# Front adjacency loads issued together, its masks made in place two chunks at a time, and 16 filler transposes left out of a graph attention kernel

## What is computed

```
h = max(layernorm(x), 0)
neib_att = tanh(neigh @ Wn1 + bn1) @ Wn2 + bn2        # 4096 x 32
value    = neigh @ Wv + bv                            # 4096 x 128
x_att    = tanh(h @ Wx1 + bx1) @ Wx2 + bx2            # 4096 x 32
ws  = leaky_relu(x_att @ neib_att.T, 0.01)            # 4096 x 4096
ws  = softmax(where(adj > 0, ws, -9e15), axis=1)
out = x + concatenate([h @ Wfx + bfx, ws @ value], axis=1)
```

## Time and profile before

| what | value |
|---|---|
| median of three runs | 489.14 us (488.77 to 489.36) |
| the profiled execution | 488.76 us |
| its span, first to last instruction | 486.8 us |
| PE, DVE, ACT, POOL busy | 96%, 88%, 84%, 53% of the span |
| granted TensorE clock, mean | 1.00 |

### The profile page before, as it was taken

One profiled execution on the slowest core, in us unless ns is written; L12 is line 12 of the kernel. 1 busy time (PEld: TensorE's weight loads), 2 busy tenths in 40 slices (PEclk: granted clock), 3 DMA queues, 4 the chain that ended last, 5 costly groups with the idle time before them and its releaser, 6 DMA issues.

```text
span 486.8 us, 10746 instructions
## 1 busy us (share of the span) xinstructions
PE 467.1 (96%) x3728; PEld 423.8 (87%) x3728; DVE 426.0 (88%) x852; ACT 410.8 (84%) x586; POOL 258.5 (53%) x361
## 2 busy tenths in 40 slices
PE   7987889999999999999999999999999999999897
PEld 7975679998899989998998989998999989988896
DVE  4678999989989999999999998989999888989654
ACT  2455898899988999899898998899889998999763
POOL 3108147844686457745685458745694555453200
PEclk9999999999999999999999999999999999999999
DMA  8944635557456754566445854476546465551000
GB/s 316 284 91 88 151 66 88 99 93 158 86 88 110 143 104 83 107 123 136 82 95 87 173 100 73 93 140 120 104 78 130 82 110 85 102 95 37 10 12 13
DMA packets 32373, 51.51 MB, mean 106 GB/s; under 512 B 2368, under 2 KB 22976, under 8 KB 32320
## 3 DMA queue, kind: packets, MB, share of 16 engines
q0 software_dynamic: 9216, 33.56, 42.1%
q1 hardware_dynamic: 22816, 17.17, 11.0%
q10 hardware_dynamic: 288, 0.10, 0.1%
HBM read 80.19 MB, written 4.19 MB: 173 GB/s over the span
## 4 chain that ended last, share of the span: by engine, by line
PE 74%; ACT 5%; issue 4%; DVE 4%; POOL 2%; DVEq 0%; ACTq 0%; POOLq 0%
PE ps_turned L936 20%; PE ps_product L957 11%; PE ps_product L959 11%; PE ps_product L958 11%; PE ps_scores L914 10%; PE ps_scores L913 6%; PE ps_product L879 3%; POOL scores L455 2%; ACT scores L551 2%; DVE pt_lo L690 2%; ACT scores L563 1%; PE ps_product L855 1%; ACT pt_hi L525 1%; PE ps_product L871 1%; DVE mask L679 1%
## 5 line engine op out<-in xcount | busy, mean ns | idle before, releaser
L690 DVE TENSOR_TENSOR pt_lo<-ps_turned,pt_hi 128x512 fp32r<-128x512 f32 x256 | 173.5, 686 | 35.3 <-ACT pt_hi L525 23.9
L455 POOL TENSOR_TENSOR scores<-scores,mask 128x512 f32<-128x512 f32 x117 | 136.2, 1164 | 118.6 <-ACT scores L551 118.4
L525 ACT ACTIVATE pt_hi<-ps_turned 128x512 fp32r<-128x512 f32 x256 | 155.4, 607 | 42.6 <-PE ps_turned L936 41.6
L957 PE MATMUL ps_product<-pt_hi,v_hi 128*128 128x256 f32 x512 | 165.0, 322 | 0.1
L936 PE MATMUL ps_turned<-ident,scores 128*128 128x128 f32 x1024 | 154.5, 273 | 2.0 <-DVE pt_lo L690 1.7
L959 PE MATMUL ps_product<-pt_lo,v_hi 128*128 128x256 f32 x512 | 144.3, 282 | 0.0
L958 PE MATMUL ps_product<-pt_hi,v_lo 128*128 128x256 f32 x512 | 144.0, 281 | 0.0
L551 ACT ACTIVATE scores<-ps_scores 128x1024 f32<-128x1024 f32 x128 | 132.1, 1032 | 10.3 <-PE ps_scores L914 10.3
L936 PEld LDWEIGHTS ps_turned<-ident,scores 128*128 128x128 f32 x1024 | 121.2, 140 | 21.6 <-DVE pt_lo L690 3.9
L563 ACT ACTIVATE scores<-scores,neg_top 128x2048 f32<-128x2048 f32 x64 | 129.1, 2018 | 0.0
L708 DVE CUSTOM_DVE_ANT_0 scores<-ps_scores,scores,top 128x1024 f32<-128x1024 f32 x96 | 122.5, 1276 | 1.1 <-ACT scores L551 0.9
(11 more groups left out here) (71 smaller groups left out, 349.4 us busy)
## 6 DMA issues: line engine op xcount, KB each, us to landing
adj_in<-in_adj POOLq DMA_DIRECT2D x60, 512.0 KB, 5.5
scores<-in_neigh_t SPq DMA_DIRECT2D x8, 512.0 KB, 7.7
x_rows<-in_x SPq DMA_DIRECT2D x7, 512.0 KB, 5.7
x_left<-in_x SPq DMA_DIRECT2D x8, 256.0 KB, 5.7
x_right<-in_x SPq DMA_DIRECT2D x16, 128.0 KB, 5.2
scores<-in_adj POOLq DMA_DIRECT2D x4, 512.0 KB, 6.6
out_h<-x_left SPq DMA_DIRECT2D x8, 256.0 KB, 2.4
out_h<-x_right SPq DMA_DIRECT2D x16, 128.0 KB, 2.4
```

The lines of the kernel that those rows point to most:

```text
L455: pool.tensor_tensor(half, half, mask[:, s % MASK_RING, BANK:CHUNK], ALU.add).then_inc(masked, 1)
L525: act.activation(pt_hi[:, (2 * b + u) % HI_RING], pt[:, u], ACT.Copy).then_inc(hi_done, 1)
L690: dve.tensor_tensor(pt_lo[:, u], pt[:, u], pt_hi[:, (2 * b + u) % HI_RING].bitcast(FP32), ALU.subtract).then_inc(lo_done, 1)
L957: pe.matmul(product_of(g), v_hi[:, block, :], high, start=block == 0, stop=False)
```

## The change

The fillers of neighbour steps 1 to 3 are left out. POOL issues the four loads of the front one behind the other once the last neighbour load has landed. The masks of the 8 front chunks are made in place in `adj_front`, two chunks in one DVE instruction, in steps 2, 3, 6 and 8 at the end of DVE's side work. PE and POOL read them there. The mask ring and its counts skip these chunks (`ring_place`). The statistics of group 1 of x come before step 0. Due steps of x's load, normalisation, `x_left`'s load and sums and `x_right`'s sum move. In DVE's step `neigh_rest` comes before `close` (which does nothing before step 14, when `neigh_rest` is over).

```
-FILL = (6, 6, 6, 4, 0, 0, 0, 0)
+FILL = (6, 0, 0, 0, 0, 0, 0, 0)
-X_LOAD = -12
+X_LOAD = -14
 X_STATS = (-6, -6, -6, -4)
 X_AGGR = -2
 X_RSTD = (-2, -2, -1, 0)
-X_NORM = (1, 3, 3, 4)
+X_NORM = (3, 4, 4, 5)
 X_TURN = (6, 8)
...
-X_LEFT_LOAD, X_SUM = 8, (13, 18)
-X_RIGHT = 14
+X_LEFT_LOAD, X_SUM = 7, (16, 19)
+X_RIGHT = 16
...
-AHEAD_STATS = 0
+AHEAD_STATS = -1
+FRONT_MASKS = (2, 3, 6, 8)
...
+        def ring_place(n):
+            return n - FRONT if n >= ADJ_RING else n
+        def made_in_front(n):
+            return ADJ_RING <= n < ADJ_RING + FRONT
+        def mask_of_chunk(n):
+            return adj_front[:, n - ADJ_RING, :] if made_in_front(n) else mask[:, ring_place(n) % MASK_RING, :]
...
             pool.wait_ge(rows_in[NEIGH_GROUPS - 1], 16)
-            load_adj(2 * LOAD)
-            pool.wait_ge(x_ahead_in, 16)
-            load_adj(3 * LOAD)
+            for p in range(FRONT // LOAD):
+                load_adj(ADJ_RING + p * LOAD)
             for i in range(NEWTON + 1):
                 rstd_of(1, i)
-            load_adj(4 * LOAD)
-            load_adj(5 * LOAD)
...
-                    act.wait_ge(mask_done, ADJ_RING + FRONT)
+                    act.wait_ge(masked, ADJ_RING + FRONT - POOL_MASKS)
...
+                if made_in_front(n):
+                    return
...
+            def front_mask(p):
+                dve.wait_ge(front_ready[p], 16)
+                pair = adj_front[:, p * LOAD:(p + 1) * LOAD, :].rearrange("p a n -> p (a n)")
+                dve.tensor_scalar(pair, pair, 0.0, MASKED, ALU.is_le, ALU.mult).then_inc(front_masked, 1)
...
             def x_work(s):
+                for p in range(FRONT // LOAD):
+                    if s == FRONT_MASKS[p]:
+                        front_mask(p)
...
-                    pe.wait_ge(mask_done, k + 1)
+                    if made_in_front(s):
+                        pe.wait_ge(front_masked, (s - ADJ_RING) // LOAD + 1)
+                    else:
+                        pe.wait_ge(mask_done, ring_place(s) + 1)
```

More of the change, by code:

```diff
@@ L201, in build @@
         front_ready = [sem(f"front_ready{i}") for i in range(FRONT // LOAD)]
-        mask_done = sem("mask_done")
+        mask_done, front_masked = sem("mask_done"), sem("front_masked")
         scored = sem("scored")
@@ L442, in step @@
                 if s % LOAD == 0 and n < STEPS and not ADJ_RING <= s < ADJ_RING + FRONT:
-                    pool.wait_ge(mask_done, s + LOAD)
+                    pool.wait_ge(mask_done, ring_place(s) + LOAD)
                     load_adj(n)
@@ L454, in step @@
                     half = scores[:, parity * TILES + tile, c * CHUNK + BANK:(c + 1) * CHUNK]
-                    pool.tensor_tensor(half, half, mask[:, s % MASK_RING, BANK:CHUNK], ALU.add).then_inc(masked, 1)
+                    pool.tensor_tensor(half, half, mask_of_chunk(s)[:, BANK:CHUNK], ALU.add).then_inc(masked, 1)
                 for i in range(NEWTON + 1):
@@ L666, in mask_of @@
             def mask_of(n):
[L668 to L679, removed]
+                if made_in_front(n):
+                    return
+                r = ring_place(n)
+                dve.wait_ge(adj_ready[r % ADJ_RING // LOAD], 16 * (r // ADJ_RING + 1))
+                if r >= MASK_RING:
+                    gone = r - MASK_RING
+                    if gone >= ADJ_RING:
+                        gone += FRONT
+                    dve.wait_ge(scored, gone + 1)
+                    if gone >= POOL_MASKS:
+                        dve.wait_ge(masked, gone + 1 - POOL_MASKS)
+                dve.tensor_scalar(mask[:, r % MASK_RING, :], adj_in[:, r % ADJ_RING, :], 0.0, MASKED, ALU.is_le,
                                   ALU.mult).then_inc(mask_done, 1)
+            def front_mask(p):
+                dve.wait_ge(front_ready[p], 16)
+                pair = adj_front[:, p * LOAD:(p + 1) * LOAD, :].rearrange("p a n -> p (a n)")
+                dve.tensor_scalar(pair, pair, 0.0, MASKED, ALU.is_le, ALU.mult).then_inc(front_masked, 1)
             def lo(s, u):
@@ L775, in step @@
                 negate(s)
+                neigh_rest(s)
                 close(s)
-                neigh_rest(s)
                 x_work(s)
@@ L912, in score @@
                 if not on_pool:
-                    pe.matmul(ps[:, s % 2, half], ident_bf16, mask[:, s % MASK_RING, half], start=True, stop=False)
+                    pe.matmul(ps[:, s % 2, half], ident_bf16, mask_of_chunk(s)[:, half], start=True, stop=False)
                 last = pe.matmul(ps[:, s % 2, half], xs[:, parity, tile * P:(tile + 1) * P],
```

## The result

The changed kernel took a median of 493.31 us (492.57 to 494.38, four executions) against 489.25 us for the kernel before on the same chip: a ratio of 1.0094, 95% interval 1.0081 to 1.0107. It is slower by 0.9%, where 488.7 us and a range of 486.2 to 490.7 were forecast. The moved due steps, which the title doesn't name, decide it. The profiled execution took 492.57 us, 3.81 more than that of before: 3.3 in the span (490.1) and 0.5 around it. (What lies around the span was 1.9 to 2.5 us in the profiled executions of all kernels here; the runs tie it to nothing.)

What follows compares the result with a forecast made beforehand. PE was taken to set the pace from step 12 on. Fillers -0.85, front of the loop -2.0 and due steps +2.4 sum to -0.45 us on 489.14: 488.7 us, range 486.2 to 490.7.

Steps and rivals of the forecast that it cites:

- The due steps of every group: +2.4 us: Main loop: PE waits for POOL's late normalisation at the turn of x, 0.4 us later in each of six groups.
- POOL's chain: POOL from step 4's addition at 201.46 through two additions and three normalisations to 207.46, plus 0.05 signal; PE waits 0.76.
- The 0.35 that comes back: Third step of a group: moving x_left's and x_right's sums on POOL returns 0.35 us that PE lost before a score.
- full price: Rival: the turn of x costs 0.8 us in each of six groups, +1.95 in all, 491.1 us; chance 0.07.
- Fillers, -0.85: Prologue: leaving out 16 filler transposes on PE brings the value layers and first score 0.85 us earlier.
- Loads, 0: Front adjacency loads issued earlier change nothing; x_ahead still lands at 26.5; POOL may be held by a fourth load.
- Front of the loop, -2.0: Early steps: paired masks of 0.7 and earlier normalisation bring x_left's sum forward; 2.0 us passes into the main loop.
- POOL blocks the front masks: Rival: front masks wait for POOL's normalisations, the loop gains nothing, +1.55, 490.7 us; chance 0.12.
- The turn doesn't hold PE: Rival: the turn of x costs PE nothing in the groups, only the front counts, -2.85, 486.3 us; chance 0.30.
- The clock falls: Rival: without fillers PE's clock falls in the prologue, +3 on the forecast, 491.7 us; chance 0.06.
- the dear ends of the last three: Slowest outcomes of the rivals on blocked front masks, the turn's full price and the falling clock, left outside the range.

Runs made afterwards that it cites:

- e9: The kernel before with only x's normalisation moved, to steps 3, 4, 4, 5 of a group: 494.8 us, ratio 1.0122.
- e3: The changed kernel with all due steps of the side work back as before; fillers out, early loads and paired masks stay: 486.92 us, ratio 0.997.
- e4: The kernel before with only the 16 later fillers left out: 487.57 us, ratio 0.9983.
- e7: e5 with the front masks made one chunk at a time instead of two per instruction: 485.85 us, ratio 0.9943.
- e2: The kernel before with only the due steps of the change (x's load and normalisation, x_left's load and sums, x_right's sum): 493.96 us, ratio 1.0107.
- e11: e7 with all 22 fillers of the kernel before: 487.04 us, ratio 0.9965.
- e8: e5 with the four front loads issued as in the kernel before: 487.39 us, ratio 0.9976.
- e1: The changed kernel with x's normalisation alone back in steps 1, 3, 3, 4 of a group: 488.68 us, ratio 1.0003.
- e5: e3 with six fillers again before neighbour step 1: 486.58 us, ratio 0.9961.
- e6: The changed kernel with the turn of x in steps 7 and 9 instead of 6 and 8: 491.25 us, ratio 1.0047.
- e10: The changed kernel with x's normalisation and x_right's sum back in their steps of before: 486.3 us, ratio 0.9953.

## Why the prediction was wrong

**The step that failed** is "The due steps of every group: +2.4 us", a term with the right mechanism and the wrong size: it measured 5.08. The place, PE's pause before the turn of x from e = 2 to 7, ended by POOL's last normalisation, is as forecast, and e9 shows that moving the normalisation alone makes the loss. Both entries of the working were off.

*POOL's chain.* The addition of step 4 started where I had it: 200.93 here is 201.46 in the time of the earlier trace rows, as step 48 comes 0.53 earlier. From there to the end of the last normalisation I summed 6.00 us; it took 6.31, and the signal 0.10 rather than 0.05. The additions are as summed (1.17, 1.16). The normalisations are not: 2.64 for two (1.44 and 1.21) and 1.38, where I took 1.22 each from the earlier trace rows. The page shows it as a mean of 1256 ns before and 1346 after. The long two are those that begin while a mask of DVE is running, here the one below and the one at 204.95 (shown in the last section):

```profile
202.02 0.41 DVE L689 TENSOR_SCALAR mask<-adj_in 128x1024 bf16<-128x1024 bf16 x1
```

The normalisation at 202.62 from which I took the 1.22 had a whole mask inside it, which began half a us after it and cost it nothing:

```profile
203.13 0.41 DVE L679 TENSOR_SCALAR mask<-adj_in 128x1024 bf16<-128x1024 bf16 x1
```

So the turn is 1.12 late instead of 0.76, and 6 x 0.36 = 2.2 us.

*The 0.35 that comes back.* It did where I had read it: step 4 of the group that I read shrank from 3.30 to 2.94 between rises. But I counted it in all six groups. In the first two, step 4 took 2.94 already before, and these groups grew by 1.07 and 0.95; the other four grew by 0.75 to 0.78, which is the 0.4 that I had and the 0.36 of POOL's chain. So the first two add 0.5, and 2.4 + 2.2 + 0.5 is the 5.08. The 0.35 isn't even fixed by the due steps: e3, e4 and e7 have the old ones, and there the same step of the same group took 2.96, and step 6 lost 0.24 instead (2.82 between rises against 2.58). The term came out above the upper bound of 4.8, "full price", too.

I had the earlier trace rows before me, where masks beside POOL took 0.54 and 1.02 in place of 0.43. I read them only as the price for DVE and never asked what the same overlap costs POOL. On a chain of five POOL instructions with no slack, that was the question. That the masks are what lengthens the normalisations rests on their times side by side; no run moved a mask alone.

**Fillers, -0.85**: measured -0.96 at step 0, within its bounds. That it is so close is partly luck: step 0 came at 32.01, 32.74 and 32.71 in e2, e9 and e11, which have all the fillers of before (32.51). The four value layers run 3.45 us apart from the first on; the fourth comes 1.09 earlier against the first, so it did not meet DVE as I had computed. The median of e4 says 1.1. **Loads, 0**: the fourth load found no room, as I had allowed, and not only the fourth; `x_ahead` landed at 29.07, not 26.5, and harmed nobody: DVE's statistics began without a wait, at 32.29. The order was worth more than 0, though: -0.6 (e8), which I had booked in the next term. **Front of the loop, -2.0**: measured -1.60. Double masks of 0.7 were right. The point that decides is `left_sum` on POOL: DVE wrote `x_left` at 46.59 where I had put "near 46", again because POOL's normalisation took 5.62 beside the masks. Rise 7 came at 49.83 and not 49.6. The two normalisations that met the double masks took 1.50 and 1.72, the two behind them 1.21 each. **Rivals**: "POOL blocks the front masks" did not happen (0.69, 0.70); its mirror image did. "The turn doesn't hold PE" was false. "The turn costs its full price", at a chance of 0.07, had the mechanism but not the size. "The clock falls" was real: two of the four executions of the changed kernel took 494.0 and 494.4 at a mean clock of 0.995 and 0.994, against 492.6 for the others, which puts 0.7 us on the median; a fall costs 1.4 us, not 3.

**The end, +0.77**, was not foreseen. PE's last work ends 2.5 later and the last store lands 0.75 later still. The DMA view from 487 to 490 us (queue, packets, MB, share; the issue and its time to landing):

```profile
q14 instruction: 1, 0.01, 1.1%
...
out_h<-x_right SPq DMA_DIRECT2D x1, 128.0 KB, 2.6
```

The same store landed in 1.81 us in before, e2, e4, e7, e9 and e11, and in 2.56 to 2.87 in the changed kernel, e1, e3, e5, e6, e8 and e10. In all of the latter, and in none of the former, a packet of the instruction queue begins 1.2 to 1.5 us after the store's issue. That goes with the store being late; I could not turn it on and off by itself, so it stays a correlation. It means that of any difference here between two of these kernels 0.75 us or more may go with where such a packet falls; e5 against e7 is such a pair.

**The range** reached 490.7 because I left out "the dear ends of the last three" rivals. The ends of the loss were correlated: POOL's slower normalisations cost in the front and in each of six groups at once. And 0.7 us of the median is the lower clock in two of four executions. With the term at 5.08, the ledger gives 488.76 - 0.96 - 1.60 + 5.08 + 0.77 + 0.5 = 492.55, the profiled execution.

## What to carry to other kernels

- A due step that repeats in every group is worth more attention than a whole prologue: one tuple here cost 5.9 us, and all work on the front gained 2.9 (e7 against before). For a chain that ends in a wait of the bounding engine, sum its instructions with the durations that they have beside their new neighbours, in both directions of the contention.
- A time "given back" that was read in one group must be looked up in each group before it is multiplied.
- A pause is best read from start to start against the same place in the other kernel; where ends are modelled, the idle time of a row is too short.
- The fastest version is e7, 485.85 us: the new front with single masks, the first two filler bursts, and all due steps as before. e10's groups are 1.1 us shorter in all than e7's, so its `X_SUM = (16, 19)` and loads on top of e7 may gain about that much more; this was not tried.

## What the runs showed of the hardware

**DVE and POOL hold each other up.** The Trainium skill, "SBUF — State Buffer", Who interferes with whom, calls the port pair that they share an exclusive lock. The trace agrees with that for one kind of neighbour. In step 5 of the group shown, DVE's mask starts 0.24 after POOL's addition (204.71, ends 205.87) and ends 0.28 after it:

```profile
204.95 1.20 DVE L689 TENSOR_SCALAR mask<-adj_in 128x1024 bf16<-128x1024 bf16 x1
```

Six masks of the changed kernel take 1.20 to 1.22 in this way, and in before five that start 0.45 after an addition take 1.00, the one of the earlier trace rows among them. A mask alone takes 0.42.

Beside a normalisation one of the two pays, and not always the same one. In the changed kernel six normalisations that begin 0.07 to 0.09 after a mask take 1.42 to 1.44 in place of 1.21, the masks 0.41 or 0.42. Where the mask begins 0.03 or 0.04 after the normalisation, it goes either way: in before four such masks take 0.78 to 0.80 and the normalisations 1.21 or 1.22, in e7 five take 0.41 to 0.45 and the normalisations 1.46 to 1.50. What decides between them is open. A lock that one of two always holds in full is not seen there: the masks of 0.8 end 0.4 before the normalisation.

**POOL had room for three adjacency loads in flight.** The fourth waited 2.3 to 3.2 us at its issue, each time until the one three before it had landed, and held POOL.

**The clock at the start is not the same in every execution.** Two things differ. One is when it first rises. The 21 transposes ahead of the first layer, which every kernel here has, took 3.87 us in e7, 4.21 in before and 4.74 in the changed kernel; in e8 the clock was still at its lower level at 10 us, which made step 0 1.6 later than in e5. The other is whether it falls again, as in e3. A fall shows in the mean clock of the execution: with all fillers from step 1 on left out, 9 of 49 executions (the changed kernel, e1, e3, e4, e6, e10) had 0.994 to 0.996 and took 1.3 to 2.2 us longer than the others of their kernel. With the burst of step 1 kept it was none of 19 (e5, e7, e8), and with all fillers none of 75 (before, e2, e9, e11). So the burst seems to hold the clock; only e3's fall was profiled, and 19 executions are few. Three executions can easily miss it.
